# Cross attention on one core: sums over eight key tiles, a third score buffer and a new order on TensorE and DVE

## The chip, the core and the metric

The kernel runs on one core of a Trainium2 chip. Its engines are TensorE (matmuls, with a part of its own for loading weights), DVE, ACT, POOL and SP, which issues transfers. Each runs its own queue in order and they meet at semaphores. The metric is the device time of one execution in microseconds. TensorE's clock has two levels here, 1.2 and 2.4 GHz, and the profile shows the granted one as a share of the full one.

## What is computed

The program is a small perceiver of two layers: x is 2 x 256 tokens of 256 features and the context is 2 x 4096 tokens. The change lies in the cross attention, which stands once in each layer. In short:

```
def cross(x, ctx):                  # 16 heads of 16 features, 2 batches
    q, k, v = heads(x @ wq), heads(ctx @ wk), heads(ctx @ wv)
    scores = einsum('bhqd,bhkd->bhqk', q, k) * 0.25 + bias   # layer 0: mask, layer 1: (q - k) * w_rel
    probs = softmax(scores, axis=-1)                          # over 4096 keys
    return einsum('bhqk,bhkd->bqhd', probs, v)
x = x + layer0_cross_block(layernorm(x), ctx)   # cross, then self attention and a dense part
x = x + clamped_attention(layernorm(x));  x = x + experts0(layernorm(x))
x = x + cross(layernorm(x), ctx) @ w_proj
x = x + self_attention(layernorm(x));     x = x + experts1(layernorm(x))
```

## The kernel before

`cross_attention` (L884) runs once a layer. It goes through 32 heads, g = 0 to 31: 16 heads times 2 batches, called heads here. The first and last four are written out, and the 24 between are a hardware loop of six rounds, four heads to a round (`all_heads`, L927). `m` is g modulo 4 and picks one of four key and query buffers (`kst`, `qst`), `b` is g modulo 2 and picks the batch.

Queries and keys hold three bf16 pieces of each fp32 value, stacked in 105 rows. A head takes two passes over its keys:

- The first pass finds the maximum of each query row. It has 8 units (L991), each two matmuls of 128 queries by 512 keys into one of two buffers of `ps1`. DVE takes the maximum of 1024 scores (`take_max`, L1103). A unit waits until the unit two before it has been taken.
- After the eighth maximum DVE splits the row maximum into three negated pieces (`c_rows`, five small instructions). TensorE turns them (`turn_c`, L1005) into `ps_m` and DVE copies them into the query stack (`copy_c`, L1115). The second pass of the head waits for that.
- The second pass computes scores again, less the maximum, turned so that keys lie in partitions. It has 16 pairs (L1012), each two matmuls of 128 keys by 256 queries into one of two buffers of `ps2`. ACT writes their exponentials into `probs`, which has 8 slots of one pair each (L1093).
- Sum groups (`pv_group`, L1024) multiply exponentials with values and ones, in fp32. Four key tiles (two pairs) are one group, each tile in its own 32 columns of TensorE, so that four partial sums stand in the four quarters of `ps_o`. There are 8 groups to a head. The profile records each fp32 matmul twice, so a group of 4 instructions has 8 records.
- When a head's last sum is done ACT copies it (`copy_o`, L1082), TensorE adds the quarters and turns them (`finish`, L1039) into `ps_m`, and DVE divides (`finish`, L1119): a reciprocal and a product.

The order is written by hand and overlaps three heads. While TensorE does the second pass of head g, it also does the first-pass units 2 to 7 of head g + 1 after pairs 1, 3, 5, 7, 8 and 10 (`PASS1_AT`, L1070), and units 0 and 1 of head g + 2 after pairs 14 and 15. The sum group of pairs 2o and 2o + 1 follows pair 2o + 3. The last group of head g - 1 follows pair 1 of head g, its output turn follows pair 5, and the turn of the maxima of g + 1 stands after pair 15. DVE takes eight maxima of g + 1, with the output of g - 1 after the fourth, then splits and copies. SP loads keys and POOL copies queries and values into place as soon as a second pass or a head's sums let them.

Of the kernel before, what the change touches and what calls it, by code (L numbers as in the profile page):

```python
# [22 lines left out]
BF16 = mybir.dt.bfloat16  # L23
# [860 lines left out]
def cross_attention(pr, buffers):  # L884
# [6 lines left out]
    W1 = SK // NC1  # L891
    N1 = QT * NC1
    N2 = KT // 2
    GROUP = 2
    NPV = N2 // GROUP
    SLOTS = 8
    CH = 5
    NK = 16 * len(K_PIECES)
    kst, qall, vall, k_in = buffers.kst, buffers.qall, buffers.vall, buffers.k_in
    with ExitStack() as st:  # L900
# [8 lines left out]
        rcp = pr.sb(st, "rcp", [P, QT])  # L909
# [12 lines left out]

        def head_number(h2, m):

# [12 lines left out]
        with nc.Block() as block:  # L937
# [50 lines left out]

            @block.tensor
            def _(pe):  # L990
                def pass1(g, m, b, u, wait=True):  # L991

                    if u == 0:

                        pe.wait_ge(k_in[m], NK // NBUF * (g - m) + NK + buffers.n_aux)
                        pe.wait_ge(q_ready, g + 1)
                    if wait:
                        pe.wait_ge(mx, N1 * g + u - 1)
                    qt, c = u // NC1, u % NC1
                    for x in range(W1 // 512):  # L1000
                        mm = pe.matmul(ps1[:, u % 2, x * 512:(x + 1) * 512], qst[:, m, qt * P:(qt + 1) * P],  # L1001
                                       kst[:, m, c * W1 + x * 512:c * W1 + (x + 1) * 512], start=True, stop=True)
                    mm.then_inc(sc1, 1)

                def turn_c(g):  # L1005

                    pe.wait_ge(c_chain, CH * g + CH)
                    for qt in range(QT):
                        mm = pe.transpose(ps_c[:, qt * P:(qt + 1) * P], cp[:, qt, :], pr.cb("identb"))  # L1009
                    mm.then_inc(c_turned, 1)  # L1010

                def pass2(g, m, b, u, wait=True):  # L1012

                    if u == 0:
                        pe.wait_ge(c_ready, g + 1)
                    if wait:
                        pe.wait_ge(probs_ready, N2 * g + u - 1)
                    for x in range(2):
                        kt = 2 * u + x
                        mm = pe.matmul(ps2[:, u % 2, x, :], kst[:, m, kt * P:(kt + 1) * P], qst[:, m, :],  # L1020
                                       start=True, stop=True)
                    mm.then_inc(sc2, 1)

                def pv_group(g, b, o, first=False):  # L1024

                    if o == 0:
                        pe.wait_ge(v_ready, g + 1)
                        if not first:
                            pe.wait_ge(o_copied, g)
                    pe.wait_ge(probs_ready, N2 * g + GROUP * (o + 1))  # L1030
                    for i in range(2 * GROUP):
                        kt = 2 * GROUP * o + i
                        j = kt % 4
                        mm = pe.matmul(ps_o[32 * j:32 * j + 32, b, :], vst[:, b, kt, :],  # L1034
                                       probs[:, (kt // 2) % SLOTS, kt % 2, :],
                                       start=(kt < 4), stop=(kt >= KT - 4), skip_group_check=True)
                    mm.then_inc(pv, 1)

                def finish(g, b, wait=True):  # L1039

                    pe.wait_ge(o_copied, g + 1)
                    if wait:
                        pe.wait_ge(o_done, 2 * g)
                    for qt in range(QT):
                        mm = pe.matmul(ps_f[:, qt, :], o_sb[:, b, qt * P:(qt + 1) * P], pr.cf("sel4"),
                                       start=True, stop=True)
                    mm.then_inc(o_turned, 1)

                def head(g, h, m, b, place):


                    last, first = place == "last", place == "first"
                    for u in range(N2):
                        pass2(g, m, b, u, wait=not (first and u < 2))
                        if u == 1 and not first:
                            pv_group(g - 1, 1 - b, NPV - 1)
                        if u > GROUP and u % GROUP == 1:
                            pv_group(g, b, u // GROUP - 1, first)
                        if u in PASS1_AT and not last:
                            pass1(g + 1, (m + 1) % NBUF, 1 - b, 2 + PASS1_AT.index(u))  # L1060
                        if u == 5 and not first:
                            finish(g - 1, 1 - b, wait=not (isinstance(g, int) and g == 1))
                        if u == N2 - 1 and not last:
                            turn_c(g + 1)
                        if u >= N2 - 2 and not last and place != "last but one":
                            pass1(g + 2, (m + 2) % NBUF, b, u - (N2 - 2))

                PASS1_AT = (1, 3, 5, 7, 8, 10)  # L1070
                for u in range(N1):
                    pass1(0, 0, 0, u, wait=u >= 2)
# [5 lines left out]
                finish(NG - 1, 1)  # L1078

            @block.scalar  # L1080
            def _(act):
                def copy_o(g, b):  # L1082
                    act.wait_ge(pv, NPV * (g + 1))
                    nc.scalar.copy(o_sb[:, b, :], ps_o[:, b, :]).then_inc(o_copied, 1)

                def head(g, h, m, b, place):
                    for u in range(N2):
                        if u == 2 and place != "first":
                            copy_o(g - 1, 1 - b)
                        act.wait_ge(sc2, N2 * g + u + 1)  # L1090
                        if u % GROUP == 0 and not (place == "first" and u < SLOTS):
                            act.wait_ge(pv, NPV * g + u // GROUP - SLOTS // GROUP + 1)
                        nc.scalar.activation(probs[:, u % SLOTS, :, :], ps2[:, u % 2, :, :], ACT.Exp).then_inc(  # L1093
                            probs_ready, 1)

                all_heads(act, head)
                copy_o(NG - 1, 1)

            @block.vector
            def _(dve):  # L1100
                v = nc.vector
                link = Chain(dve, c_chain)
                def take_max(g, b, u):  # L1103
                    dve.wait_ge(sc1, N1 * g + u + 1)
                    v.tensor_reduce(top[:, b, u // NC1, u % NC1:u % NC1 + 1], ps1[:, u % 2, :], AX, ALU.max).then_inc(  # L1105
                        mx, 1)

                def c_rows(g, b):
# [9 lines left out]

                def finish(g, h, b):  # L1119
                    dve.wait_ge(o_turned, g + 1)  # L1120
                    v.reciprocal(rcp[:, :], ps_f[:, :, DH]).then_inc(o_done, 1)
                    dve.wait_ge(o_done, 2 * g + 1)
                    v.tensor_tensor(pr.attn[:, :, b, ds(h * DH, DH)], ps_f[:, :, 0:DH], bc(rcp[:, :], 2, DH),
                                    ALU.mult).then_inc(o_done, 1)

                def head(g, h, m, b, place):

                    before = (g - 1, h - 1 if b == 0 else h, 1 - b)
                    if place == "last":
                        finish(*before)  # L1130
                        return
                    for u in range(N1):
                        take_max(g + 1, 1 - b, u)
                        if u == 3 and place != "first":
                            finish(*before)
                    c_rows(g + 1, 1 - b)
                    copy_c(g + 1, (m + 1) % NBUF)

                for u in range(N1):
                    take_max(0, 0, u)  # L1140
                c_rows(0, 0)
                copy_c(0, 0)
                all_heads(dve, head)
                finish(NG - 1, H - 1, 1)
# [1381 lines left out]
```

## Time and profile before

| | us |
|---|---|
| median of 3 runs | 1944.72 |
| lowest and highest run | 1944.52, 1946.14 |
| profiled execution, its own time | 1940.99 |
| its span | 1939.1 |
| busy TensorE matmul, DVE, ACT in the span | 1710.2, 1122.6, 867.0 |
| cross attention of layer 0, about | 266 to 705 |
| cross attention of layer 1, about | 1272 to 1709 |

Everything else lies outside of these two stages: projecting the context ahead of the first, the rest of layer 0 between them, and the rest of layer 1 behind the second. A row of the order of time gives start, length, engine, line, tile written and tiles read, operand shapes and count; several instructions of one kind in a row are merged into one row with one length. The recorded lengths of matmuls overlap, so the time that a piece costs is the distance from its start to the start of what follows. In brackets stands idle time of the engine before the row, and what ended it.

### The profile page before, as it was taken

The page shows a single profiled execution, that of the slowest core. Times are in us where ns is not written, and L with a number is a line of the kernel's source. Part 1 is how long each engine was busy: PE and PEld are TensorE (multiplying, and loading weights), DVE is VectorE, ACT ScalarE, POOL GpSimd, SP SyncE. Part 2 cuts the span into 40 slices and gives each one's busy share as a digit, 9 for nine tenths or more (in the row PEclk, how much of TensorE's full clock was granted, in tenths as well). Part 3 has the DMA queues.
Part 4 walks back from the last instruction along what each step waited for, and adds up shares of the span by engine and source line. Part 5 has one row for each costly group of instructions (what it writes and reads, how often), then busy time and mean ns, then how long its engine had stood idle before and what let it go on. Part 6 is the DMA issues. An engine that isn't in the chain of part 4 may idle for free. (4 is left out here: it accounts for less than half of the span.)

```text
span 1939.1 us, 35950 instructions
## 1 busy us (share of the span) xinstructions
PE 1710.2 (88%) x12064; PEld 955.7 (49%) x12064; DVE 1122.6 (58%) x1947; ACT 867.0 (45%) x1734; POOL 180.0 (9%) x271
## 2 busy tenths in 40 slices
PE   7999969999999969758948999279999999978697
PEld 4444424444444436435828888124444444445587
DVE  5777758888788846346440000368888888726301
ACT  2222227666666746303411111037666667736222
POOL 1321210000000000001112000310000000000000
PEclk9999969999999989879968999679999999989699
DMA  5587684344344220000086999434344344130142
GB/s 188 182 210 204 183 182 77 56 59 65 49 65 62 37 98 1 1 1 0 1 217 217 314 312 322 133 60 66 55 60 65 51 62 63 19 89 1 52 145 76
DMA packets 146010, 198.69 MB, mean 102 GB/s; under 512 B 26104, under 2 KB 119137, under 8 KB 139549
## 3 DMA queue, kind: packets, MB, share of 16 engines
q1 hardware_dynamic: 142324, 193.54, 41.6%
q0 software_dynamic: 1536, 2.17, 0.4%
q10 hardware_dynamic: 2064, 1.87, 0.3%
q8 instruction: 51, 0.84, 0.2%
q14 instruction: 35, 0.28, 0.1%
HBM read 159.08 MB, written 43.11 MB: 104 GB/s over the span
## 5 line engine op out<-in xcount | busy, mean ns | idle before, releaser
L1093 ACT ACTIVATE probs<-ps 128x512 f32<-128x512 f32 x1024 | 573.9, 596 | 287.3 <-PE ps L1020 276.2
L1105 DVE TENSOR_REDUCE top<-ps 128x1 f32<-128x1024 f32 x512 | 600.9, 1218 | 35.5 <-PE ps L1001 33.1
L1001 PE MATMUL ps<-kst,qst 105*128 105x512 bf16 x1024 | 318.8, 394 | 36.5 <-POOL qst L959 28.5
L1020 PE MATMUL ps<-qst,kst 105*128 105x256 bf16 x2048 | 344.0, 275 | 2.3 <-DVE qst L1117 1.8
L1034 PE MATMUL ps_o<-probs,vst 128*32 128x256 f32 x4096 | 328.5, 392 | 0.8 <-ACT probs L1093 0.8
L1020 PEld LDWEIGHTS ps<-qst,kst 105*128 105x128 bf16 x2048 | 176.2, 100 | 215.2 <-ACT probs L1093 64.8
L1001 PEld LDWEIGHTS ps<-kst,qst 105*128 105x128 bf16 x1024 | 66.0, 98 | 190.4 <-DVE top L1105 90.0
L1034 PEld LDWEIGHTS ps_o<-probs,vst 128*32 128x32 f32 x4096 | 80.7, 108 | 109.7 <-issue 88.4
L1942 PE MATMUL ps_h<-xe,wgu 128*128 128x80 f32 x1024 | 126.7, 285 | 1.8 <-issue 1.0
L1942 PEld LDWEIGHTS ps_h<-xe,wgu 128*128 128x128 f32 x1024 | 123.4, 201 | 3.4 <-issue 2.5
L488 PE MATMUL ps_k<-ctxT,wk 128*128 128x512 f32 x256 | 122.2, 600 | 1.1 <-DVE square_weights L653 1.1
L496 PE MATMUL ps_v<-wv,ctxT 128*128 128x512 f32 x256 | 120.4, 592 | 0.0
L2087 DVE TENSOR_TENSOR hT<-silu,ps_h 128x320 f32<-128x320 f32 x32 | 15.6, 488 | 171.0 <-ACT silu L1999 171.0
L965 POOL COPY vst<-vall 128x512 f32 (+1 forms) x64 | 39.1, 613 | 768.2 <-PE ps_o L1034 768.1
L569 ACT COPY vall<-ps_v 128x256 f32 (+1 forms) x64 | 23.8, 372 | 176.8 <-PE ps_v L496 176.8
L744 PE MATMUL ps_t<-consts,xn 128*128 128x128 f32 x56 | 13.8, 428 | 89.9 <-DVE xn L694 51.5
L652 DVE TENSOR_SCALAR kp<-ps_k,kbias 128x512 bf16<-128x512 f32 x64 | 48.0, 750 | 56.9 <-PE ps_k L488 56.5
L496 PEld LDWEIGHTS ps_v<-wv,ctxT 128*128 128x128 f32 x256 | 48.9, 191 | 61.8 <-issue 61.8
L488 PEld LDWEIGHTS ps_k<-ctxT,wk 128*128 128x128 f32 x256 | 47.9, 192 | 56.0 <-issue 50.1
L1117 DVE COPY qst<-ps_m 3x256 bf16<-3x256 bf16 x64 | 18.1, 283 | 86.3 <-PE ps_m L1009 86.3
L605 POOL TENSOR_TENSOR vall<-vall,L_xattn_cv_b 128x256 f32 (+1 forms) x64 | 48.8, 762 | 195.6 <-ACT square_weights L571 195.2
L1999 ACT ACTIVATE silu<-ps_h 128x320 f32<-128x320 f32 x32 | 14.0, 437 | 110.8 <-PE ps_h L1942 110.8
(333 smaller groups left out, 1846.3 us busy)
## 6 DMA issues: line engine op xcount, KB each, us to landing
kst<-kd SPq DMA_DIRECT2D x384, 128.0 KB
kd<-kp SPq DMA_DIRECT2D x64, 384.0 KB, 2.8
wgu<-in_L_ffn_wg_dram SPq DMA_DIRECT2D x32, 512.0 KB, 4.8
wgu<-in_L_ffn_wu_dram SPq DMA_DIRECT2D x32, 512.0 KB, 6.7
wd<-in_L_ffn_wd_dram SPq DMA_DIRECT2D x32, 512.0 KB, 6.8
w<-in_L_ffn_w_dram SPq DMA_DIRECT2D x16, 1024.0 KB, 5.6
ctx_sb<-in_ctx_dram SPq DMA_DIRECT2D x16, 512.0 KB, 5.9
vd<-square_weights SPq DMA_DIRECT2D x16, 512.0 KB, 4.1
```

The costliest lines, as they stand in the source:

```text
L488: mm = pe.matmul(ps_k[:, q % 2, :], wk[:, c, q // C, (q % C) * P:(q % C + 1) * P], ctxT[:, par, c, :], start=(c == 0), stop=(c == C - 1))
L496: mm = pe.matmul(ps_v[:, t % 2, :], ctxT[:, par, c, t * P:(t + 1) * P], wv[:, c, :, :].rearrange("p l d -> p (l d)"), start=(c == 0), stop ...
L569: nc.scalar.copy(buffers.vall[:, ds(n * TB + t, 1), :].rearrange("p o d -> p (o d)"), ps_v[:, t % 2, 0:D])
L605: g.tensor_tensor(v, v, pr.row["L0_xattn_cv_b"][:, :], ALU.add).then_inc(v_bias, 1)
L652: link(v.tensor_scalar(kp[:, q, 0, :], ps_k[:, q % 2, :], b, None, ALU.add))
L965: nc.gpsimd.tensor_copy(vst[:, b, :, 0:DH], vall[:, b * KT:(b + 1) * KT, ds(h * DH, DH)]).then_inc(v_ready, 1)
L1001: mm = pe.matmul(ps1[:, u % 2, x * 512:(x + 1) * 512], qst[:, m, qt * P:(qt + 1) * P], kst[:, m, c * W1 + x * 512:c * W1 + (x + 1) * 512], ...
L1020: mm = pe.matmul(ps2[:, u % 2, x, :], kst[:, m, kt * P:(kt + 1) * P], qst[:, m, :], start=True, stop=True)
L1034: mm = pe.matmul(ps_o[32 * j:32 * j + 32, b, :], vst[:, b, kt, :], probs[:, (kt // 2) % SLOTS, kt % 2, :], start=(kt < 4), stop=(kt >= KT ...
L1093: nc.scalar.activation(probs[:, u % SLOTS, :, :], ps2[:, u % 2, :, :], ACT.Exp).then_inc(probs_ready, 1)
L1105: v.tensor_reduce(top[:, b, u // NC1, u % NC1:u % NC1 + 1], ps1[:, u % 2, :], AX, ALU.max).then_inc(mx, 1)
L1942: mm = pe.matmul(hview[:, b, i, f, :], wgu[:, b, i, c, f * P:(f + 1) * P], xe[:, b, c, :], start=(c == 0), stop=(c == C - 1))
```

## The change

All of it is in `cross_attention`.

- `GROUP` is 4: a sum group covers four pairs, eight key tiles, and a head has 4 groups of 8 instructions.
- `ps2` has three buffers. `SCORES2` gives the buffer of each pair (0, 1, 2 in turn, and 1 for pair 15). A pair waits for the exponential that last read its buffer: three pairs back as a rule, two for pairs 1 and 15, four for pairs 0 and 2.
- The eight PSUM banks are shared out anew. `ps_m` is gone. The turned maxima go into `ps2` buffer 0, so `turn_c` also waits for exponential 12 of the head in the second pass. The turned output goes into the buffer of `ps1` that unit 4 used, so `finish` on TensorE waits for maximum 4. Unit 6 takes the buffer of unit 5 and waits for maximum 5, and unit 7 waits until DVE has read the output. `ps_o` has one buffer for both batches.
- On TensorE the units of g + 1 follow pairs 0, 1, 2, 5, 9 and 10, those of g + 2 follow pairs 11 and 15, the sum groups follow pairs 6, 11 and 13 and pair 0 of the next head, the output turn follows pair 7, the turned maxima follow pair 14.
- DVE takes maximum 0 of head g + 2 between the split and the copy of the turned maxima, and the output after maximum 5.
- ACT copies the last head's sum ahead of exponential 1, not 2.

```diff
-    GROUP = 2
+    GROUP = 4
+    SCORES2 = (0, 1, 2, 0, 1, 2, 0, 1, 2, 0, 1, 2, 0, 1, 2, 1)
+    EARLIER2 = tuple(next(d for d in range(1, N2) if SCORES2[(u - d) % N2] == SCORES2[u]) for u in range(N2))
+    C_SLOT, C_AFTER = 0, 12
...
-        ps2 = pr.ps(st, "ps2", [P, 2, 2, S])
-        ps_o = pr.ps(st, "ps_o", [P, B, S])
-        ps_m = pr.ps(st, "ps_m", [P, 512])
-        ps_c = ps_m[0:NPIECE, 0:P].bitcast(BF16)
-        ps_f = ps_m[:, 256:256 + QT * 64].rearrange("p (t d) -> p t d", t=QT)
+        ps2 = pr.ps(st, "ps2", [P, 3, 2, S])
+        ps_o = pr.ps(st, "ps_o", [P, 512])[:, 0:S]
+        ps_c = ps2[0:NPIECE, C_SLOT, 0, 0:P].bitcast(BF16)
+        ps_f = [ps1[:, x, 0:QT * 64].rearrange("p (t d) -> p t d", t=QT) for x in range(2)]
...
+        def slot1(m, u):
+            return (m + u + 1 + (u >= 6)) % 2
...
-                    if wait:
+                    if u == 6:
+                        pe.wait_ge(mx, N1 * g + u)
+                    elif u == 7 and finished:
+                        pe.wait_ge(o_done, 2 * (g - 1))
+                    elif wait:
                         pe.wait_ge(mx, N1 * g + u - 1)
...
                     pe.wait_ge(c_chain, CH * g + CH)
+                    if not (isinstance(g, int) and g == 0):
+                        pe.wait_ge(probs_ready, N2 * (g - 1) + C_AFTER + 1)
...
-                        pe.wait_ge(probs_ready, N2 * g + u - 1)
+                        pe.wait_ge(probs_ready, N2 * g + u - EARLIER2[u] + 1)
...
-                        if u == 1 and not first:
+                        if u in SUMS_AT and SUMS_AT.index(u) < NPV - 1:
+                            pv_group(g, b, SUMS_AT.index(u), first)
+                        if u == FINISH_AT and not first:
+                            finish(g - 1, 1 - b, ahead=not last)
+                        if u in PASS1_AT and not last:
+                            pass1(g + 1, (m + 1) % NBUF, 1 - b, 2 + PASS1_AT.index(u), finished=not first)
+                        if u in NEXT_AT and not last and place != "last but one":
+                            pass1(g + 2, (m + 2) % NBUF, b, NEXT_AT.index(u))
+                        if u == SUMS_AT[-1] and not first:
                             pv_group(g - 1, 1 - b, NPV - 1)
...
+                SUMS_AT, FINISH_AT, TURN_AT = (6, 11, 13, 0), 7, 14
+                PASS1_AT, NEXT_AT = (0, 1, 2, 5, 9, 10), (11, 15)
...
-                        if u == 2 and place != "first":
+                        if u == 1 and place != "first":
                             copy_o(g - 1, 1 - b)
...
-                    for u in range(N1):
-                        take_max(g + 1, 1 - b, u)
-                        if u == 3 and place != "first":
+                    for u in range(1, N1):
+                        take_max(g + 1, (m + 1) % NBUF, 1 - b, u)
+                        if u == 5 and place != "first":
                             finish(*before)
                     c_rows(g + 1, 1 - b)
+                    if place != "last but one":
+                        take_max(g + 2, (m + 2) % NBUF, b, 0)
                     copy_c(g + 1, (m + 1) % NBUF)
```

In the orders below `ps_97` is the first-pass buffer `ps1` and `ps_98` the score buffer `ps2`. TensorE from score pair 0 of head 1 on, before:

```order
L1020 MATMUL ps_98<-qst,kst 128x256 x4
L1034 MATMUL ps_o<-probs,vst 32x256 x4
L1001 MATMUL ps_97<-kst,qst 128x512 x2
L1020 MATMUL ps_98<-qst,kst 128x256 x4
L1034 MATMUL ps_o<-probs,vst 32x256 x4
L1001 MATMUL ps_97<-kst,qst 128x512 x2
L1020 MATMUL ps_98<-qst,kst 128x256 x4
L1034 MATMUL ps_o<-probs,vst 32x256 x4
L1001 MATMUL ps_97<-kst,qst 128x512 x2
L1045 MATMUL ps_m<-consts,o_sb 128x64 x2
```

The same engine and place now, up to the output turn (x6 are three pairs in a row):

```order
L1012 MATMUL ps_97<-kst,qst 128x512 x2
L1047 MATMUL ps_o<-probs,vst 32x256 x8
L1033 MATMUL ps_98<-qst,kst 128x256 x2
L1012 MATMUL ps_97<-kst,qst 128x512 x2
L1033 MATMUL ps_98<-qst,kst 128x256 x2
L1012 MATMUL ps_97<-kst,qst 128x512 x2
L1033 MATMUL ps_98<-qst,kst 128x256 x6
L1012 MATMUL ps_97<-kst,qst 128x512 x2
L1033 MATMUL ps_98<-qst,kst 128x256 x2
L1047 MATMUL ps_o<-probs,vst 32x256 x8
L1033 MATMUL ps_98<-qst,kst 128x256 x2
L1061 MATMUL ps_97<-consts,o_sb 128x64 x2
```

One pair stands ahead of the first row. Three first-pass units are issued by pair 2 where before one was, two large sum groups stand where three small ones did, and the output turn writes a first-pass buffer.

TensorE at the end of a head, before, from the last sum groups to the next head's pairs 0 and 1:

```order
L1034 MATMUL ps_o<-probs,vst 32x256 x4
L1020 MATMUL ps_98<-qst,kst 128x256 x2
L1001 MATMUL ps_97<-kst,qst 128x512 x2
L1020 MATMUL ps_98<-qst,kst 128x256 x2
L1034 MATMUL ps_o<-probs,vst 32x256 x4
L1009 MATMUL ps_m<-constsb,cp 3x128 x2
L1001 MATMUL ps_97<-kst,qst 128x512 x2
L1020 MATMUL ps_98<-qst,kst 128x256 x4
```

The same place now, from sum group 1 to the next head's pair 0 and unit 2:

```order
L1047 MATMUL ps_o<-probs,vst 32x256 x8
L1012 MATMUL ps_97<-kst,qst 128x512 x2
L1033 MATMUL ps_98<-qst,kst 128x256 x4
L1047 MATMUL ps_o<-probs,vst 32x256 x8
L1033 MATMUL ps_98<-qst,kst 128x256 x2
L1022 MATMUL ps_98<-constsb,cp 3x128 x2
L1033 MATMUL ps_98<-qst,kst 128x256 x2
L1012 MATMUL ps_97<-kst,qst 128x512 x2
L1033 MATMUL ps_98<-qst,kst 128x256 x2
L1012 MATMUL ps_97<-kst,qst 128x512 x2
```

Unit 0 of the head after next moved up by three pairs, and the turned maxima stand ahead of pair 15 and write a score buffer. DVE from one copy of turned maxima to the split of the next head, before:

```order
L1117 COPY qst<-ps_m 3x256
L1105 TENSOR_REDUCE top<-ps_97 128x1 x4
L1121 RECIPROCAL rcp<-ps_m 128x2
L1123 TENSOR_TENSOR attn<-ps_m,rcp 128x2x16
L1105 TENSOR_REDUCE top<-ps_97 128x1 x4
L1112 TENSOR_REDUCE cwhole<-top 128x2
```

The same now, with the maximum ahead of the copy as its first row:

```order
L1122 TENSOR_REDUCE top<-ps_97 128x1
L1134 COPY qst<-ps_98 3x256
L1122 TENSOR_REDUCE top<-ps_97 128x1 x5
L1138 RECIPROCAL rcp<-ps_97 128x2
L1140 TENSOR_TENSOR attn<-ps_97,rcp 128x2x16
L1122 TENSOR_REDUCE top<-ps_97 128x1 x2
L1129 TENSOR_REDUCE cwhole<-top 128x2
```

One of the eight maxima moved ahead of the copy, and the output from behind the fourth to behind the sixth.

## Rows read from the trace of the kernel before

**Rows 1.** Stretches: length, busy time (and records) by engine, clock, DMA share, GB/s.

```profile
278.24:293.05 14.81, 14.59 (x102) 5.72 (x103) 10.32 (x13) 8.76 (x16) 0.00 (x0) 0.75 0.98 239
293.05:691.56 398.51, 395.59 (x3542) 170.13 (x3538) 323.82 (x480) 277.15 (x511) 28.01 (x58) 1.00 0.38 56
1297.99:1695.49 397.50, 395.62 (x3543) 170.20 (x3538) 323.33 (x480) 277.16 (x511) 28.00 (x58) 1.00 0.37 56
599.21:612.86 13.65, 13.29 (x122) 5.65 (x118) 10.86 (x16) 9.25 (x18) 0.96 (x2) 1.00 0.38 58
612.86:626.06 13.20, 13.20 (x122) 5.68 (x118) 10.77 (x16) 9.22 (x18) 0.96 (x2) 1.00 0.43 60
```

**Rows 2.** Order of time on TensorE, most of one head and the turn after.

```profile
604.86 0.56 PE L1045 MATMUL ps_m<-consts,o_sb 128*128 128x64 f32 x4
605.25 0.60 PE L1020 MATMUL ps<-qst,kst 105*128 105x256 bf16 x4
605.78 0.64 PE L1034 MATMUL ps_o<-probs,vst 128*32 128x256 f32 x8
606.35 0.60 PE L1001 MATMUL ps<-kst,qst 105*128 105x512 bf16 x2
606.79 0.38 PE L1020 MATMUL ps<-qst,kst 105*128 105x256 bf16 x2
607.33 0.60 PE L1001 MATMUL ps<-kst,qst 105*128 105x512 bf16 x2 [0.16 <-DVE top L1105]
607.77 0.38 PE L1020 MATMUL ps<-qst,kst 105*128 105x256 bf16 x2
608.09 0.64 PE L1034 MATMUL ps_o<-probs,vst 128*32 128x256 f32 x8
608.66 0.39 PE L1020 MATMUL ps<-qst,kst 105*128 105x256 bf16 x2
608.89 0.59 PE L1001 MATMUL ps<-kst,qst 105*128 105x512 bf16 x2
...
612.86 0.28 PE L1009 MATMUL ps_m<-constsb,cp 128*3 128x128 bf16 x2
613.07 0.60 PE L1001 MATMUL ps<-kst,qst 105*128 105x512 bf16 x2
613.59 0.61 PE L1020 MATMUL ps<-qst,kst 105*128 105x256 bf16 x4
```

**Rows 3.** Order of time on DVE in the same head, from its first maximum.

```profile
600.04 4.69 DVE L1105 TENSOR_REDUCE top<-ps 128x1 f32<-128x1024 f32 x4 [0.23 <-PE ps L1001]
605.45 0.17 DVE L1121 RECIPROCAL rcp<-ps_m 128x2 f32<-128x2 f32 x1 [0.71 <-PE ps_m L1045]
...
606.05 4.69 DVE L1105 TENSOR_REDUCE top<-ps 128x1 f32<-128x1024 f32 x4
610.78 0.16 DVE L1112 TENSOR_REDUCE cwhole<-top 128x2 f32<-128x8 f32 x1
...
611.58 0.16 DVE L761 TENSOR_TENSOR cp<-crest,cp 128x2 bf16<-128x2 f32 x1
613.17 0.28 DVE L1117 COPY qst<-ps_m 3x256 bf16<-3x256 bf16 x1 [1.44 <-PE ps_m L1009]
613.49 2.35 DVE L1105 TENSOR_REDUCE top<-ps 128x1 f32<-128x1024 f32 x2
```

**Rows 4.** Order of time: a unit and its maximum, an exponential after its pair.

```profile
286.99 0.60 PE L1001 MATMUL ps<-kst,qst 105*128 105x512 bf16 x2
...
287.64 3.49 DVE L1105 TENSOR_REDUCE top<-ps 128x1 f32<-128x1024 f32 x3 [0.32 <-PE ps L1001]
...
608.19 0.60 ACT L1093 ACTIVATE probs<-ps 128x512 f32<-128x512 f32 x1 [0.30 <-PE ps L1020]
```

**Rows 5.** Order of time on TensorE in the self attention of layer 0.

```profile
762.27 1.07 PE L1277 MATMUL ps_o<-pT,vst 128*32 128x256 f32 x16
763.27 1.09 PE L1263 MATMUL ps_t<-consts,probs 128*128 128x128 f32 x8
```

More of the change, by code:

```diff
@@ L990, in _, with pass1 @@
             def _(pe):
-                def pass1(g, m, b, u, wait=True):
+                def pass1(g, m, b, u, wait=True, finished=True):
                     if u == 0:
@@ L1033, in pv_group @@
                         j = kt % 4
-                        mm = pe.matmul(ps_o[32 * j:32 * j + 32, b, :], vst[:, b, kt, :],
+                        mm = pe.matmul(ps_o[32 * j:32 * j + 32, :], vst[:, b, kt, :],
                                        probs[:, (kt // 2) % SLOTS, kt % 2, :],
@@ L1037, in pv_group, with finish @@
                     mm.then_inc(pv, 1)
-                def finish(g, b, wait=True):
+                def finish(g, b, ahead=True):
                     pe.wait_ge(o_copied, g + 1)
-                    if wait:
+                    if ahead:
+                        pe.wait_ge(mx, N1 * (g + 2) + 5)
+                    else:
+                        pe.wait_ge(mx, N1 * NG)
                         pe.wait_ge(o_done, 2 * g)
                     for qt in range(QT):
-                        mm = pe.matmul(ps_f[:, qt, :], o_sb[:, b, qt * P:(qt + 1) * P], pr.cf("sel4"),
+                        mm = pe.matmul(ps_f[1 - b][:, qt, :], o_sb[:, b, qt * P:(qt + 1) * P], pr.cf("sel4"),
                                        start=True, stop=True)
@@ L1053, in head @@
                     for u in range(N2):
-                        pass2(g, m, b, u, wait=not (first and u < 2))
-                        if u == 1 and not first:
-                            pv_group(g - 1, 1 - b, NPV - 1)
[L1057 to L1063, printed above, removed]
+                        pass2(g, m, b, u, wait=not (first and u < 3))
+                        if u in SUMS_AT and SUMS_AT.index(u) < NPV - 1:
[7 more added lines that the diff above has]
+                        if u == SUMS_AT[-1] and not first:
+                            pv_group(g - 1, 1 - b, NPV - 1)
+                        if u == TURN_AT and not last:
                             turn_c(g + 1)
-                        if u >= N2 - 2 and not last and place != "last but one":
-                            pass1(g + 2, (m + 2) % NBUF, b, u - (N2 - 2))
-                PASS1_AT = (1, 3, 5, 7, 8, 10)
+                SUMS_AT, FINISH_AT, TURN_AT = (6, 11, 13, 0), 7, 14
+                PASS1_AT, NEXT_AT = (0, 1, 2, 5, 9, 10), (11, 15)
                 for u in range(N1):
-                    pass1(0, 0, 0, u, wait=u >= 2)
+                    pass1(0, 0, 0, u, wait=u >= 2, finished=False)
                 for u in range(2):
@@ L1077, in _ @@
                 pv_group(NG - 1, 1, NPV - 1)
-                finish(NG - 1, 1)
+                finish(NG - 1, 1, ahead=False)
             @block.scalar
@@ L1092, in head @@
                             act.wait_ge(pv, NPV * g + u // GROUP - SLOTS // GROUP + 1)
-                        nc.scalar.activation(probs[:, u % SLOTS, :, :], ps2[:, u % 2, :, :], ACT.Exp).then_inc(
+                        nc.scalar.activation(probs[:, u % SLOTS, :, :], ps2[:, SCORES2[u], :, :], ACT.Exp).then_inc(
                             probs_ready, 1)
```

19 lines of the change are left out of this document (10 added, 9 removed).

## The prediction

> **What bounds the kernel now.** I read the stretches first. The change touches only the two cross-attention stages. Between the second turned maximum of a stage and its last one lie 30 heads, 398.51 us in layer 0 and 397.50 us in layer 1, both at a granted clock of 1.00 [rows 1]. That is (398.51 + 397.50) / 60 = 13.27 us a head, and 64 such heads are over two fifths of the span. An ordinary head in a hardware loop takes 13.20 us and the first head of a loop round 13.65 us. In the ordinary one TensorE is busy for all 13.20 us, DVE for 10.77 and ACT for 9.22 [rows 1]. A busy matmul row is no proof of a full TensorE, since starts are what counts; so the next view is the order of time of one head, in which I take prices from start to start [rows 2].
>
> - A score pair (two matmuls) before another pair is 0.21 us, before a first-pass unit 0.23, before a sum group 0.32: 608.66 to 608.89, 607.77 to 608.09, and 0.53 for two pairs ahead of a sum at 605.25.
> - So the step from scores into a sum group costs 0.32 - 0.21 = 0.11 us. A sum group over four key tiles is 0.57 us (608.09 to 608.66).
> - A first-pass unit is 0.44 (606.35 to 606.79), the output's turn 0.39 (604.86 to 605.25), the turned maxima 0.21 (612.86 to 613.07).
>
> The sum per head is 16 x 0.215 + 8 x 0.44 + 8 x (0.57 + 0.11) + 0.39 + 0.21 = 13.0 us. TensorE is therefore nearly full, and what it waits for are maxima: at 606.79 a pair takes 0.54 us, since the unit behind it starts only when DVE is done with that buffer. DVE is nearly as tight [rows 3]. Four maxima run from 606.05 to 610.78, 1.18 us each. Then the three parts of the maximum take until 611.75, DVE waits 1.44 us for the turn on TensorE, and copies until 613.45. A wait of 0.71 us stands before the reciprocal. A maximum starts 0.65 us after its unit does (286.99 to 287.64), and an exponential 0.42 us after its pair [rows 4]. DVE and TensorE thus take turns in holding the head up, and a gain on one is worth only what the other lets through.
>
> **Eight tiles to a sum.** Four groups of 8 instructions replace eight of 4. The trace holds a group of this size elsewhere: the self attention's 16 recorded matmuls of 128x256 fp32 with 32 columns take 1.00 us from start to start [rows 5], against 0.57 for 8 here. So half a group more costs 0.43 us and the way out of a group 0.14. With the 0.11 on the way in a boundary costs 0.25, and four fewer save 8 x 0.68 - 4 x 1.11 = 1.00 us of TensorE a head. TensorE's own work falls to 12.0 us. One of the four groups now follows a first-pass unit, which no row shows; between nothing and 0.22 us (twice the step from a pair) I take 0.11, since the operand shapes are those of a pair.
>
> The Trainium skill (TensorE: Matmul & The Clock Gate, Step-by-step: what each phase is for) says that TensorE pulls weight loads ahead of running matmuls. By that rule alone a boundary would cost nothing and this part would save nothing, not 1.00 us. The starts at 607.77 and 608.09, 0.32 where 0.21 is a pair, show a cost at the boundary; I go by them.
>
> **Third score buffer.** It makes a pair wait for the exponential three pairs back, not two. An exponential is done 0.42 + 0.60 = 1.02 us after its pair starts. In the new order three pairs stand in a row twice (0.21 apart). With two buffers they would stall there, with three they don't by my layout: pair 5 is due 1.1 us after pair 2. Its last pair has only two back, 1.7 us. I cost it at nothing. Its cover is the slack of 0.1 us at pair 5; if the exponentials run later by d, TensorE loses d - 0.1.
>
> **The new order, laid out.** Zero is score pair 0 of a head. On TensorE: pair 0, unit 2 at 0.23, the old head's last sum at 0.78, pair 1 at 1.78, unit 3 at 2.00, pair 2, unit 4 (2.7), pairs 3 to 5, unit 5, pair 6, sum 0, pair 7, output turn, pairs 8 and 9, unit 6, pair 10, unit 7, pair 11, sum 1, the unit 0 after next, pairs 12 and 13, sum 2, pair 14, turned maxima, pair 15, unit 1. Against it DVE has maxima 1 to 5, the output, maxima 6 and 7, the three parts, maximum 0 of the head after, the copy. The chain that closes the head is:
>
> 1. TensorE from pair 0 to unit 3: 2.00 us.
> 2. Unit 3's maximum must be done before unit 5, which has its buffer: 0.65 + 1.18 + 0.10 = 1.93. (0.10 is from the maximum's end at 607.23 to the unit at 607.33.) TensorE alone would need 1.75, so it stalls 0.18.
> 3. TensorE from unit 5 to unit 6: 0.44 + 0.32 + 1.00 + 0.21 + 0.39 + 0.21 + 0.23 = 2.80.
> 4. Handoff to maximum 6: 0.65.
> 5. DVE: 3 x 1.18 + 0.97 + 0.30 = 4.81, and 0.14 from the copy's end to the next pair 0 (613.45 to 613.59).
>
> Together 12.33 us. Maximum 0 in place of the turn's wait is what the move buys: before, DVE idles there; now it works 1.18 us and the turn (11.4) is ready when it ends. The turn's new wait on exponential 12 has pairs 15 and 0 and a unit queued behind it on TensorE, but pair 12 starts at 9.6, so that exponential ends by 10.7. The output turn now stands in a first-pass buffer. It waits for maximum 4 (done at 5.0, turn at 5.9), and unit 7 waits for DVE's read of it (done by 7.1, unit due at 7.4). Unit 6 has the buffer of unit 5 and waits for that maximum (6.2, due 6.7). The single sum buffer makes sum 0 wait for ACT's copy, now one exponential earlier, done at about 2.3 and needed at 4.7. Behind unit 0 on TensorE all of the next head queues, and unit 0 is wanted three pairs sooner than before, while SP's key loads and POOL's query and value copies start from the same events as before. In the head shown TensorE waits for a maximum alone [rows 2], so I cost the three pairs (under 3 us with the sum between) at nothing; they cost what a load is later than that.
>
> What the loop adds (13.20 against 13.65 at its edge, where DVE takes 0.23 us longer to start [rows 3]) falls on DVE just after the copy and in the output step. There the new layout leaves it idle 0.3 to 0.4 us. I keep 0.07 of it as a mean and take 12.40 us a head. That saves 13.27 - 12.40 = 0.87, times 60 = 52 us. Against it, each stage's first copy now stands behind a maximum, about 0.3 us net of a group boundary saved, and 0.2 us for the last, larger sum at the end, where its 0.43 us lies bare: 1 us for both stages. **Net 51 us.** The profiled execution would go from 1940.99 to 1890; it lies 3.7 us under the median, so the forecast for the median is 1944.7 - 51 = 1893.7 us.
>
> **Rivals.**
>
> - TensorE alone sets the head. For it: 12.0 us of work, and my stall of 0.18 and the end of the chain hang on a tenth or two. Against: the chain is already laid out without loss. 12.0 us a head gives 76 - 1 = 75 us: 1870.
> - The handoffs stay bare. For it: the loop's edge costs 0.45 us now, 0.11 a head; if that falls on a busy DVE, with the unit-to-sum step at its bound (0.11 more), and the exponentials at pair 5 and the output's round trip through a first-pass buffer each late by 0.1 us, it is 12.33 + 0.42, near 12.8 us. That gives 28 - 1 = 27 us: 1918. Against: the idle time in the layout.
> - A sum over eight tiles costs two of four, less little, so that the part doesn't do what it says: 13.0 us a head, 1930. Against: the 1.00 us row.
> - Slower: the granted clock. New pauses of TensorE before unit 5 and pair 0, once each a head, let the clock fall. The head at a mean clock of 0.75 took 14.81 us, 1.54 more than the mean head, half of it at 1.2 GHz [rows 1]. It decides from the point where a loss of 0.87 us a head eats the gain, which is 0.87 / 1.54 of that, a mean clock of 0.86. At 0.75 throughout, 12.40 + 1.54 = 13.94 us a head, 60 x 0.67 = 40 us slower: 1985. Against: the clock stands at 1.00 over both stretches with stalls of 0.1 to 0.3 us in every head. The Trainium skill (same page, A second HAM failure mode: psum-queue depth-cycling) tells of a kernel whose micro-idles between groups, as it goes round its PSUM buffers, made the clock swing. This trace shows such pauses without the swing.
>
> **How the numbers follow.** Forecast 0.61 (own range 1884 to 1905), TensorE alone 0.13, bare handoffs 0.18 (1905 to 1930), no cheaper sums 0.03, clock 0.05. Up to 1920 and down to 1872 some 0.8 is held. A measurement of this kernel can tell about 0.2%, 4 us, from no change. Faster 0.93, same 0.02 (the upper end of the bare handoffs), slower 0.05.
>
> **What would show it.** Right: turned maxima 12.3 to 12.5 us apart, sum groups of 16 records at 1.00 us, a first-pass unit stalled by some 0.2 us on its maximum once a head, DVE's wait before the copy of turned maxima near nothing and its busy share above 85%, clock 1.00. Wrong: a copy on DVE that waits over 0.3 us for the turn, a score pair that waits for an exponential, or sum groups well over 1.00 us. The forecast fails most easily in the chain of five steps, since a tenth of a microsecond in it is 6 us of the program.

## The result

| | before | changed |
|---|---|---|
| median of 4 runs, us | 1945.43 | 1897.57 |
| lowest and highest, us | 1944.52, 1947.2 | 1895.45, 1898.05 |
| profiled execution, us | 1940.99 | 1897.33 |
| 30 heads of layer 0 and of layer 1, us | 398.51, 397.50 | 373.95, 374.14 |

The ratio is 0.9743, with a 95% interval of 0.9725 to 0.9762. The changed kernel is 47.9 us faster. The forecast was 1893.7 us, so the gain came out 3 us under the 51 of the sum. The granted clock was 1.00 over both stretches, as before.

The stretches of the changed kernel, with the columns of [rows 1]: the 30 heads of each layer between the second and the last turned maxima, then one written-out head and one head of the hardware loop.

```profile
294.14:668.09 373.95, 371.84 (x3539) 185.59 (x3538) 326.09 (x480) 271.03 (x510) 28.00 (x58) 1.00 0.40 60
1279.67:1653.81 374.14, 371.76 (x3540) 185.67 (x3540) 326.13 (x480) 270.96 (x510) 28.01 (x58) 1.00 0.39 59
318.82:331.16 12.34, 12.32 (x120) 6.19 (x120) 10.89 (x17) 9.07 (x17) 0.96 (x2) 1.00 0.45 66
606.38:618.89 12.51, 12.42 (x119) 6.20 (x118) 10.89 (x17) 9.02 (x17) 0.95 (x2) 1.00 0.41 63
```

The mean head is (373.95 + 374.14) / 60 = 12.47 us, where [rows 1] give 13.27. DVE is busy for 326 of 374 us, 87%. There are two kinds of head now: 12.34 us where they are written out, 12.51 in the loop. The edge of the loop, 13.65 against 13.20 us in [rows 1], no longer shows: of 24 looped heads in layer 0 none was over 12.52 us, and in layer 1 one took 12.69.

The order of time on TensorE in the written-out head, from the turned maxima to unit 6, answers to [rows 2]:

```profile
318.82 0.27 PE L1022 MATMUL ps<-constsb,cp 128*3 128x128 bf16 x2
...
319.74 0.39 PE L1033 MATMUL ps<-qst,kst 105*128 105x256 bf16 x2
319.97 0.59 PE L1012 MATMUL ps<-kst,qst 105*128 105x512 bf16 x2
320.50 1.07 PE L1047 MATMUL ps_o<-probs,vst 128*32 128x256 f32 x16
321.50 0.39 PE L1033 MATMUL ps<-qst,kst 105*128 105x256 bf16 x2
321.73 0.59 PE L1012 MATMUL ps<-kst,qst 105*128 105x512 bf16 x2
...
322.81 0.82 PE L1033 MATMUL ps<-qst,kst 105*128 105x256 bf16 x6
323.64 0.60 PE L1012 MATMUL ps<-kst,qst 105*128 105x512 bf16 x2
...
326.46 0.59 PE L1012 MATMUL ps<-kst,qst 105*128 105x512 bf16 x2
```

A sum group over eight tiles takes 1.00 us, from 320.50 to 321.50, and behind a unit it starts 0.53 us after it, a step of 0.09. Pairs 3 to 5 take 0.83 us up to unit 5, where 0.65 is their own, so unit 5 stalls 0.18 us for maximum 3.

DVE in the same head, which answers to [rows 3]:

```profile
319.40 0.28 DVE L1134 COPY qst<-ps 3x256 bf16<-3x256 bf16 x1
319.88 5.96 DVE L1122 TENSOR_REDUCE top<-ps 128x1 f32<-128x1024 f32 x5 [0.20 <-PE ps L1012]
326.22 0.17 DVE L1138 RECIPROCAL rcp<-ps 128x2 f32<-128x2 f32 x1 [0.38 <-PE ps L1061]
...
327.09 2.36 DVE L1122 TENSOR_REDUCE top<-ps 128x1 f32<-128x1024 f32 x2 [0.48 <-PE ps L1012]
329.48 0.16 DVE L1129 TENSOR_REDUCE cwhole<-top 128x2 f32<-128x8 f32 x1
...
330.28 0.16 DVE L761 TENSOR_TENSOR cp<-crest,cp 128x2 bf16<-128x2 f32 x1
330.48 1.22 DVE L1122 TENSOR_REDUCE top<-ps 128x1 f32<-128x1024 f32 x1
331.74 0.28 DVE L1134 COPY qst<-ps 3x256 bf16<-3x256 bf16 x1
```

The wait of 1.44 us before the copy is gone: maximum 0 fills it, and the copy follows without idle time. What DVE idles in the head is 0.20 + 0.38 + 0.48 us, each for TensorE.

### The profile page after: what moved, and what is told of

Its sections match the earlier page's. It is cut to its first block and busy times, and to the rows that moved or that the text cites. A ratio compares the mean times of both kernels' runs of the same rounds, so it can differ in the third digit from the quotient of the medians.

```text
span 1895.5 us, 35714 instructions
## 1 busy us (share of the span) xinstructions
PE 1657.8 (87%) x12064; PEld 989.1 (52%) x12064; DVE 1129.2 (60%) x1947; ACT 853.4 (45%) x1734; POOL 180.0 (9%) x271
## 5 line engine op out<-in xcount | busy, mean ns | idle before, releaser
L1110 ACT ACTIVATE probs<-ps 128x512 f32<-128x512 f32 x1024 | 558.5, 600 | 204.3 <-PE ps L1033 191.9
L1033 PE MATMUL ps<-qst,kst 105*128 105x256 bf16 x2048 | 354.3, 276 | 7.7 <-DVE qst L1134 2.4
L1033 PEld LDWEIGHTS ps<-qst,kst 105*128 105x128 bf16 x2048 | 170.2, 100 | 228.1 <-ACT probs L1110 85.9
L1047 PE MATMUL ps_o<-probs,vst 128*32 128x256 f32 x4096 | 274.1, 385 | 2.3 <-ACT probs L1110 2.3
L1047 PEld LDWEIGHTS ps_o<-probs,vst 128*32 128x32 f32 x4096 | 106.8, 109 | 113.4 <-issue 51.5
L1012 PEld LDWEIGHTS ps<-kst,qst 105*128 105x128 bf16 x1024 | 90.1, 99 | 102.3 <-issue 59.8
L1974 PE MATMUL acc<-wd,hT 128*80 128x256 f32 x256 | 61.9, 386 | 0.0
```

Source lines behind the costliest of these rows:

```text
L1012: mm = pe.matmul(ps1[:, slot1(m, u), x * 512:(x + 1) * 512], qst[:, m, qt * P:(qt + 1) * P], kst[:, m, c * W1 + x * 512:c * W1 + (x + 1) * ...
L1033: mm = pe.matmul(ps2[:, SCORES2[u], x, :], kst[:, m, kt * P:(kt + 1) * P], qst[:, m, :], start=True, stop=True)
L1047: mm = pe.matmul(ps_o[32 * j:32 * j + 32, :], vst[:, b, kt, :], probs[:, (kt // 2) % SLOTS, kt % 2, :], start=(kt < 4), stop=(kt >= KT - 4 ...
L1110: nc.scalar.activation(probs[:, u % SLOTS, :, :], ps2[:, SCORES2[u], :, :], ACT.Exp).then_inc(probs_ready, 1)
L1974: mm = pe.matmul(ps_y[0:CAP0, b, :], hT[:, b, f, :], wd[:, b, f, :], start=(f == 0), stop=(f == FT0 - 1))
```

## Experiments

All are edits of the changed kernel, save the one with the old order, which is an edit of the kernel before. Heads are read from one turn of the maxima to the next. Ratios are against runs of the kernel before on the same chip, whose median lay between 1947.8 and 1951.8 us in these comparisons; so times of different comparisons differ by a few microseconds for that alone, and ratios and head lengths are what to compare.

| kernel | median us | ratio (95%) | head written out | head in the loop |
|---|---|---|---|---|
| changed | 1897.57 | 0.9743 (0.9725 to 0.9762) | 12.34 | 12.51 |
| old order, sums over eight | 1999.63 | 1.0270 (1.0249 to 1.0291) | 14.00 | 14.14 |
| new order, sums over four | 1982.29 | 1.0171 (1.0147 to 1.0196) | 13.79 | 13.86 |
| the same, one sum later | 1964.61 | 1.0069 (1.0046 to 1.0092) | 13.58 | 13.58 |
| two score buffers | 1947.86 | 1.0001 (0.9989 to 1.0014) | 13.04 | 13.22 |
| maximum 0 after the copy | 1937.03 | 0.9947 (0.9929 to 0.9965) | 13.17 | 13.10 |
| no loop | 1893.07 | 0.9696 (0.9679 to 0.9713) | 12.34 | none |
| no loop on DVE | 1893.68 | 0.9698 (0.9680 to 0.9716) | 12.34 | 12.41 |
| no loop on TensorE | 1898.78 | 0.9727 (0.9708 to 0.9745) | 12.34 | 12.45 |
| unit 6 after pair 8 | 1888.64 | 0.9676 (0.9654 to 0.9697) | 12.27 | 12.30 |
| the same, no loop | 1886.58 | 0.9680 (0.9657 to 0.9703) | 12.27 | none |
| unit 6 after pair 8, unit 3 ahead of pair 1 | 1891.74 | 0.9699 (0.9678 to 0.9719) | 12.34 | 12.38 |

**The larger sums alone.** The kernel before with one edit:

```diff
-    GROUP = 2
+    GROUP = 4
```

> The kernel before with GROUP = 4 alone: two score buffers, the old order. My theory (TensorE and DVE hand each other the head, so a lighter TensorE alone helps little): TensorE's work falls by 1.0 us a head, but DVE still does four maxima, the output, four maxima, the split and then waits for the turn; laid out with the same prices the head closes at about 13.1 us (unit 6 waits for maximum 4, the copy of turned maxima stands behind the last sums), 1930 to 1945 us in all. Rival (TensorE's work is what counts): about 12.3 us a head, 1885 to 1895 us.

Measured: 2.7% slower than before, 14.14 us a looped head. Both theories missed. Mine expected a slightly shorter head, 13.1 us, and the rival a much shorter one; TensorE has 1.0 us less to do, and the head is 0.9 us longer. One looped head of it on TensorE, and DVE beside it:

```profile
507.68 0.88 PE L1020 MATMUL ps<-qst,kst 105*128 105x256 bf16 x4
508.49 1.07 PE L1034 MATMUL ps_o<-probs,vst 128*32 128x256 f32 x16
...
511.40 0.39 PE L1020 MATMUL ps<-qst,kst 105*128 105x256 bf16 x2
512.41 0.60 PE L1001 MATMUL ps<-kst,qst 105*128 105x512 bf16 x2 [0.62 <-DVE top L1105]
...
514.83 0.81 PE L1020 MATMUL ps<-qst,kst 105*128 105x256 bf16 x4
515.90 0.39 PE L1020 MATMUL ps<-qst,kst 105*128 105x256 bf16 x2 [0.26 <-ACT probs L1093]
516.22 1.07 PE L1034 MATMUL ps_o<-probs,vst 128*32 128x256 f32 x16
```

```profile
510.53 0.17 DVE L1121 RECIPROCAL rcp<-ps_m 128x2 f32<-128x2 f32 x1 [1.19 <-PE ps_m L1045]
...
518.51 0.28 DVE L1117 COPY qst<-ps_m 3x256 bf16<-3x256 bf16 x1 [1.25 <-PE ps_m L1009]
```

The two pairs at 507.68 take 0.81 us up to the sum where 0.53 is their own, and the three from 514.83 take 1.39 instead of 0.75: with a sum only every fourth pair, pairs stand closer together, and with two buffers they wait for exponentials. The pair at 511.40 takes 1.01 us instead of 0.23, since the unit behind it waits for a maximum. DVE is late there: it idled 1.19 us ahead of the reciprocal, where 0.71 stood [rows 3]. The output turn starts 5.32 us after pair 0, before the change 4.92 with a wait of 0.28 for a maximum in it: two large sums (2.01 us) stand there for three small ones (1.71), and the pairs at 507.68 have waited. The waits at 507.68, 514.83 and 511.40 are 0.28 + 0.64 + 0.78 = 1.7 of the 2.0 us by which the head exceeds TensorE's work of 12.1 (that figure is the 12.27 us of a TensorE-bound head below, less its stall of 0.18). In my layout of this kernel I had the wait for the maximum, but not the exponentials. No run gives the old order the third buffer beside the larger sums, so how much of the rest of the new order would then still be needed is not measured.

**The order and the third buffer without the larger sums.**

```diff
-    GROUP = 4
+    GROUP = 2
...
-                SUMS_AT, FINISH_AT, TURN_AT = (6, 11, 13, 0), 7, 14
+                SUMS_AT, FINISH_AT, TURN_AT = (3, 5, 7, 9, 11, 13, 15, 0), 7, 14
```

> The changed kernel with GROUP = 2: sums over four key tiles again, after pairs 3, 5, 7, 9, 11, 13, 15 and 0, everything else as changed. My theory: TensorE's work is 1.0 us a head more, 13.0 us, and with the step of the loop the head takes 13.1 to 13.4 us, 1935 to 1950 us. Rival (the order and the third buffer bring the gain, the size of the sums little): 12.5 to 12.7 us a head, 1898 to 1910 us.

Measured: 1.7% slower than before, 13.86 us. The rival falls: the order brings nothing without the larger sums. But my size was short by 0.5 us, and the orders show why. Ahead of unit 6 now stand five small groups, 5 x 0.68 = 3.4 us, where the changed kernel has two large ones, 2.2. That is 1.2 us more on the chain that closes the head, of the 1.35 by which it is longer. To test that reading I moved one group behind unit 6:

```diff
-                SUMS_AT, FINISH_AT, TURN_AT = (3, 5, 7, 9, 11, 13, 15, 0), 7, 14
+                SUMS_AT, FINISH_AT, TURN_AT = (3, 5, 7, 10, 11, 13, 15, 0), 7, 14
```

> As e2 (the changed order with sums over four key tiles), but the fifth of the eight sum groups counted from pair 0 follows pair 10 in place of pair 9, so that four small groups, not five, stand ahead of unit 6. In e2 the head took 13.86 us, since the chain from pair 0 to unit 6 grew by 1.3 us. My theory (the chain from TensorE over unit 6 to DVE closes the head, and a small group costs 0.68 us of it): the head is shorter by one group, 13.1 to 13.3 us, and the program by 36 to 45 us, to some 1937 to 1946. Rival (small groups cost by their number wherever they stand): no change, 13.86 us.

Measured: 13.58 us. The place of a group counts, so the rival (their number alone) falls, but the move gave 0.28 us and not 0.68. The chain stopped being the bound on the way: with five groups ahead TensorE waits 0.44 us for DVE at the turned maxima and at pair 0, and 0.27 at unit 4; with four the first two waits are gone and the one at unit 4 is 0.42. TensorE around unit 4 then:

```profile
512.10 0.38 PE L1033 MATMUL ps<-qst,kst 105*128 105x256 bf16 x2
512.32 0.59 PE L1012 MATMUL ps<-kst,qst 105*128 105x512 bf16 x2
512.84 0.64 PE L1047 MATMUL ps_o<-probs,vst 128*32 128x256 f32 x8
...
514.07 0.38 PE L1033 MATMUL ps<-qst,kst 105*128 105x256 bf16 x2
514.71 0.60 PE L1012 MATMUL ps<-kst,qst 105*128 105x512 bf16 x2 [0.26 <-DVE top L1122]
```

The pair at 514.07 takes 0.64 us instead of 0.22: a last sum of 0.57 us instead of 1.00 brings TensorE to unit 4 before DVE has done maximum 2. Without this 0.42 TensorE's own steps in the head are 13.16 us, against 12.09 in the TensorE-bound kernel with large sums below. The small sums thus cost about 1.07 us of TensorE a head, near the 1.00 that the prediction gave to four boundaries. The Trainium skill (TensorEngine Tiling (Array Packing), Key Properties) says that a change of the tiling mode drains TensorE; the 0.11 us into a group of 32-column tiles [rows 2] and the 0.14 out of it, worked out from [rows 2] and [rows 5], agree with that, though no run here tells a drain from another cost of the change.

**Two score buffers.** The third holds only the turned maxima.

```diff
-    SCORES2 = (0, 1, 2, 0, 1, 2, 0, 1, 2, 0, 1, 2, 0, 1, 2, 1)
+    SCORES2 = (0, 1) * 8
...
-    C_SLOT, C_AFTER = 0, 12
+    C_SLOT, C_AFTER = 2, 12
...
-                        pass2(g, m, b, u, wait=not (first and u < 3))
+                        pass2(g, m, b, u, wait=not (first and u < 2))
```

> The changed kernel with two score buffers in turn (the third buffer holds only the turned maxima). My theory: in the row of pairs 3, 4, 5 each waits for the exponential two back, pair 5 by some 0.5 us, and all behind it is late by that: 13.0 us a head, 1925 to 1935 us, with TensorE's weight loads of scores waiting for ACT. Rival (the exponentials are early enough, the third buffer is idle): 12.5 us a head, 1897 us.

Measured: 13.22 us in the loop, the time of the kernel before. The theory holds, and its rival falls. The size was short by 0.2 us. TensorE in a looped head:

```profile
510.45 0.81 PE L1033 MATMUL ps<-qst,kst 105*128 105x256 bf16 x4
511.52 0.39 PE L1033 MATMUL ps<-qst,kst 105*128 105x256 bf16 x2 [0.26 <-ACT probs L1110]
511.75 0.59 PE L1012 MATMUL ps<-kst,qst 105*128 105x512 bf16 x2
...
514.12 0.85 PE L1033 MATMUL ps<-qst,kst 105*128 105x256 bf16 x4
514.81 0.59 PE L1012 MATMUL ps<-kst,qst 105*128 105x512 bf16 x2
```

Pairs 3 to 5 take 1.30 us in place of 0.83, and pairs 8 and 9, which I had not counted, 0.69 in place of 0.44. Together that is the 0.71 us between 12.51 and 13.22.

**Maximum 0 after the copy.**

```diff
-                    for u in range(1, N1):
+                    for u in range(N1):
                         take_max(g + 1, (m + 1) % NBUF, 1 - b, u)
...
-                    if place != "last but one":
-                        take_max(g + 2, (m + 2) % NBUF, b, 0)
...
-                take_max(1, 1, 1, 0)
```

> The changed kernel with DVE's maximum 0 of the next head but one taken after the copy of turned maxima again, as before the change. My theory: DVE then idles 0.5 to 0.7 us for the turn ahead of the copy, and unit 2 waits about 1.0 us for maximum 0: 13.0 us a head, 1925 to 1940 us. Rival (DVE has slack in the new order, since it idles before maxima 1, 6 and the reciprocal anyway): under 12.7 us a head, below 1910 us.

Measured: 13.10 us for most heads of the loop, 13.17 for written-out ones and 13.30 at the loop's edge. The rival (slack on DVE) falls. TensorE and then DVE at one turn of the maxima:

```profile
503.23 0.38 PE L1033 MATMUL ps<-qst,kst 105*128 105x256 bf16 x2
504.27 0.61 PE L1012 MATMUL ps<-kst,qst 105*128 105x512 bf16 x2 [0.66 <-DVE top L1122]
```

```profile
515.78 0.28 DVE L1134 COPY qst<-ps 3x256 bf16<-3x256 bf16 x1 [1.02 <-PE ps L1022]
```

Unit 2 starts 1.04 us after pair 0, 0.81 more than a pair takes. The wait before the copy is back with 1.02 us, where I expected 0.5 to 0.7, and with it the price of the loop's edge. Why most looped heads are 0.07 us shorter here than written-out ones is open.

**Without the loop.** For the engines named, the 24 heads in the middle are written out too; work and order are the same. The edit of the first of the three kernels is shown; the other two have the last lines for DVE alone and for TensorE alone.

```diff
+        written_out = []
+
...
-            with eng.Fori(1, NG // NBUF - 1) as h2:
-                for m in range(NBUF):
-                    body(*head_number(h2, m), "")
+            if eng in written_out:
+                for h2 in range(1, NG // NBUF - 1):
+                    for m in range(NBUF):
+                        body(*head_number(h2, m), "")
+            else:
+                with eng.Fori(1, NG // NBUF - 1) as h2:
+                    for m in range(NBUF):
+                        body(*head_number(h2, m), "")
...
+                written_out.append(pe)
...
+                written_out.append(act)
...
+                written_out.append(dve)
```

> The changed kernel with all 32 heads written out for TensorE, ACT and DVE in place of the hardware loop (the work and its order are the same; SP and POOL keep their loops). In the changed kernel written-out heads take 12.34 us and looped ones 12.51. My theory: the 0.17 us come from register steps on the closing chain (one on DVE between the split and maximum 0, one on TensorE before score pair 0), so all heads take 12.34 us and the program about 8 us less, 1889 to 1891. Rival (looped heads are later for another reason, the key loads or POOL's copies, which run only there): no change, 1897; or the longer program makes engines wait for their instructions, and it is slower.

> As e5, but DVE alone is written out. If DVE's register step is the larger part (0.11 us between the split and maximum 0), heads take 12.40 us and the program 5 us less than the changed kernel, about 1892; if TensorE's steps are, 12.5 us and no change.

> As e5, but TensorE alone is written out. By the same reading (0.06 to 0.08 us before score pair 0) heads take 12.43 to 12.45 us, 3 to 4 us less than the changed kernel, about 1894; if all of it is TensorE's, 12.34 us and 1889.

Measured: all heads 12.34 us without any loop; 12.41 with DVE's loop alone gone, 12.45 with TensorE's alone gone. So 0.10 us of the 0.17 are DVE's and 0.06 to 0.07 are TensorE's, and they add up. ACT's loop adds nothing that could be seen. The rivals, a loop that is late for the transfers' or POOL's sake or a longer program that makes the heads slower, fall: SP and POOL kept their loops. The changed kernel's DVE in a looped head, and then the kernel whose DVE has no loop, show the place:

```profile
618.02 0.16 DVE L761 TENSOR_TENSOR cp<-crest,cp 128x2 bf16<-128x2 f32 x1
618.33 1.23 DVE L1122 TENSOR_REDUCE top<-ps 128x1 f32<-128x1024 f32 x1
```

```profile
514.82 0.16 DVE L761 TENSOR_TENSOR cp<-crest,cp 128x2 bf16<-128x2 f32 x1
515.02 1.23 DVE L1129 TENSOR_REDUCE top<-ps 128x1 f32<-128x1024 f32 x1
```

From the last part to maximum 0 are 0.31 us in the loop and 0.20 outside. In the loop the awaited count depends on the head, and the trace has a register instruction between the two, at 618.22, that the written-out head lacks. TensorE has one ahead of pair 0: that pair starts 0.14 us after the copy's end in the loop and 0.06 outside. In whole times the step is small: 0.9696 against 0.9743 as ratios, some 9 us, where the 60 heads of the two stretches together became 8.7 us shorter. These two intervals do not overlap. The split between the engines rests on the heads: with DVE's loop alone gone the program gained as much as without any (0.9698), where the 60 heads give 5.2 us, and with TensorE's alone gone the interval overlaps that of the changed kernel.

**Unit 6 one pair earlier.**

```diff
-                PASS1_AT, NEXT_AT = (0, 1, 2, 5, 9, 10), (11, 15)
+                PASS1_AT, NEXT_AT = (0, 1, 2, 5, 8, 10), (11, 15)
```

> The changed kernel with first-pass unit 6 after pair 8 in place of pair 9, nothing else. My theory (the closing chain runs from TensorE over the handoff to maximum 6 and from there along DVE): that handoff comes 0.21 us earlier, maximum 5 is done by then, and each head is 0.2 us shorter: 12.3 us, 1884 to 1887 us. Rival (TensorE's own work and its stall before unit 5 are the bound): no change, 1897.

Measured: 12.30 us in the loop, ratio 0.9676. The closing chain is as I laid it out: 0.21 us earlier at the handoff to maximum 6 are 0.21 us at the end of the head. The rival falls. Written out the head is 12.27 us, where TensorE itself has become the bound, with 12.09 us of work and the stall before unit 5. This kernel is faster than the changed one, and its interval overlaps that of the version without a loop (heads of 12.30 against 12.34 us). Its own version without loops was expected at 12.27 us in all heads and no time that can be told apart:

> e8 and e5 together: unit 6 after pair 8, all heads written out. In e8 written-out heads take 12.27 us, full of TensorE's own work and its stall before unit 5, and looped ones 12.30. So 12.27 us in all, about 1.5 us under e8, which a comparison can hardly tell; if the loop's 0.17 us came back in full it would be 12.13 us and 8 us less.

Measured: 12.27 us in every head but the first and the last of a stage, ratio 0.9680 against 0.9676. One thing stands out: in the profiled executions of the two kernels with all heads written out, the part behind the last turn of the maxima took 249.1 and 248.0 us at a mean granted clock of 0.87 and 0.89, in all others 241.7 to 245.5 us at 0.89 to 0.91. Two executions cannot tell chance from a price of the longer program. The last edit went for the stall of unit 5:

```diff
                         if u == SUMS_AT[-1] and not first:
                             pv_group(g - 1, 1 - b, NPV - 1)
+                        if u == 0 and not last:
+                            pass1(g + 1, (m + 1) % NBUF, 1 - b, 3, finished=not first)
...
-                PASS1_AT, NEXT_AT = (0, 1, 2, 5, 8, 10), (11, 15)
+                PASS1_AT, NEXT_AT = (0, None, 2, 5, 8, 10), (11, 15)
```

> e8 with unit 3 ahead of pair 1, right behind the last sum of the head before. It starts 0.22 us earlier, so maximum 3 is done in time and the stall of 0.18 us before unit 5 goes. If that stall were all, the head took 12.1 us, 11 us less than e8. My theory: pair 1 is now 0.44 us later, its exponential too, and pair 5 waits about 0.25 us for exponential 2, so the head takes 12.3 to 12.4 us and nothing is won: the third buffer's slack was under 0.3 us.

Measured: 12.38 us in the loop, no gain, as expected. TensorE from pairs 3 to 5 on:

```profile
506.65 1.08 PE L1033 MATMUL ps<-qst,kst 105*128 105x256 bf16 x6
507.57 0.59 PE L1012 MATMUL ps<-kst,qst 105*128 105x512 bf16 x2
```

The three pairs take 0.92 us where 0.83 stood with the stall and 0.65 is their own. The wait for maximum 3 has become one for an exponential.

## Why the prediction was right, and where it was off

- **Bound.** The reading of TensorE and DVE as holding the head by turns was right. Taken back alone, maximum 0 ahead of the copy costs 0.6 us a looped head, the third buffer 0.7 and the larger sums 1.35, where the whole change gained 0.8 in the mean: three quarters of the gain or more than all of it. The larger sums alone make the old kernel slower.
- **Sum over eight tiles.** A group was forecast at 1.00 us and measured at 1.00; the step behind a unit forecast 0.11, measured 0.09. The part was forecast to save 1.00 us of TensorE a head, and the kernels with small sums give about 1.07. It is worth that only because the rest lets it through.
- **Third buffer.** Costed at nothing with a slack of 0.1 us, and right: in the changed kernel pairs 3 to 5 stand 0.22 us apart, and the wait behind them is unit 5's for a maximum. It was closer than forecast: exponential 2 ends at 323.18 and pair 5 starts at 323.25, 0.07 us later, and in the experiment with unit 3, where pair 5 does wait, it starts 0.06 after the exponential's end.
- **The closing chain.** Forecast 12.33 us with a stall of 0.18 at unit 5; measured 12.34 and 0.18 in written-out heads. The handoff to maximum 6 is 0.63 us for a forecast 0.65, and where the prediction left DVE idle for 0.3 to 0.4 us, 0.20 stand just after the copy, 0.38 ahead of the reciprocal and 0.48 behind the output. That 12.33 met 12.34 so closely has luck in it: the 0.14 us from copy to pair 0 came from a looped head and is 0.06 in a written-out one, while DVE's part of the chain, summed as 4.81, took 4.93 (327.09 to 332.02).
- **The mis-sized term** is the loop: "I keep 0.07 of it as a mean." The edge did fall where DVE idles and vanished, as argued. But an ordinary looped head pays 0.17 us, 0.10 of it between the last part of the maximum and maximum 0, where the prediction looked just after the copy and at the output. The new order itself put that wait for a count of the head there, on the chain without slack. The mean head is 12.47, not 12.40: 0.07 x 60 = 4 us.
- **The ends.** Forecast 1 us of loss. In layer 0 the stretch from the first unit to the second turn went from 27.15 to 26.17 us, in layer 1 from 25.99 to 27.07, and from the last turn of the maxima to the last output turn from 12.55 to 13.37 and from 12.55 to 13.36. These add up to 1.7 us. The last part alone, forecast at 0.2 us a stage, took 0.8 more; no run says why. By the profile the two stages thus gained 47.9 - 1.7 = 46.2 us for a forecast of 51; the profiled executions as wholes moved by 43.7 and the medians by 47.9, and the rest lies outside of the two stages and in the spread between executions, some 2 to 3 us here. What I had not seen is in the first head: unit 6 has the buffer of unit 5 and waits 1.3 us for its maximum.
- **Rivals.** TensorE alone (12.0 us) is the bound only with unit 6 after pair 8 and the heads written out, and then stands at 12.27. The bare handoffs (12.8), no cheaper sums (13.0) and the clock, at 1.00 over both stretches, did not come.

## What to carry over

Where two engines hand the same step back and forth, lay out the chain with start-to-start prices and look for the waits; a cut in one engine's work can make the program slower (by 2.7% here) if the order around it stays. Here the larger sums alone made the program 2.7% slower, the new order and the third buffer without them 1.7% slower, and all together 2.6% faster, so judge such changes together. Inside a hardware loop look for what depends on the round on the chain without slack: a register step of 0.1 us there was paid in every head, while ACT's loop cost nothing that could be seen.

## What the runs showed of the hardware

- A written-out head repeats to 0.01 us over the heads of a stage, the first and the last left out (12.34 and 12.33 without the loop), so that one head of a trace says what a change of 0.02 us is worth.
- Writing out the 24 looped heads for three engines cost the heads no time (12.34 us in all); what it does behind them is open.
- The register step of the loop costs a head 0.10 us where it stands ahead of DVE's maximum 0 and 0.06 to 0.07 ahead of TensorE's pair 0, and the two add up to the 0.17 us.
